# Key parts copied straight to their rows of the stack, in 16 SBUF-to-SBUF transfers a batch

## The chip, the cores and the metric

The kernel runs on one core of a Trainium2 chip. The core has TensorE (matrix products), VectorE, ScalarE and GpSimd (work on rows of up to 128 partitions), SyncE, which here only issues transfers, and 16 DMA engines, which carry them. Everything between engines is ordered by semaphores that the program sets and waits for. The metric is device time in microseconds of one execution, as the median of several.

## What is computed

32 sequences of 112 tokens with 256 features (`x`) attend to contexts of 375 tokens (`ctx_1024`) and then pass a second layer. Cut to what matters for the change, which is the first half, the cross-attention with 16 heads of 16 dims:

```python
qh = _split_heads(layernorm(x) @ wq + bq)        # 32 x 16 heads x 112 x 16
kh = _split_heads(ctx @ wk + bk)                 # 32 x 16 heads x 375 x 16
vh = _split_heads(ctx @ wv + bv)
logits = jnp.einsum('bhqd,bhkd->bhqk', qh, kh) / jnp.sqrt(jnp.float32(D))
attn = jax.nn.softmax(logits + mask * -1e9, axis=-1)
x = x + jnp.tanh(g_xattn[0]) * (merge_heads(attn @ vh) @ wo + bo)
x = x + jnp.tanh(g_ffn[0]) * second_layer(layernorm(x))   # routed attention with experts
```

## The kernel before

`prepare` loads weights and constants, `cross` is the first half (all 32 batches of the cross-attention), `switch` the second layer. The change is in `cross` alone. All loops are unrolled; `batches` (L315) calls an engine's `body` once a batch, and each engine's program is an order written out by hand. TensorE's `body` (L501) mixes four batches' worth of work: the scores of batch b (`S_`, one matmul a head, L437), the turned probabilities and their product with the values (`turn` L446, `weigh` L460), the end of batch b - 1 (`heads_back`, `heads_turn`, `project`), and the context transposes, keys and queries of batch b + 2.

A score keeps float32 precision by splitting. Keys and queries are each written as a sum of three bf16 parts, and one matmul over 128 rows adds eight products of parts: `K_stack` and `Q_stack` hold, for each head, eight blocks of 16 rows (D = 16 dims). `STACKED = ((0, 3, 1), (3, 3, 2), (6, 2, 0))` says it: blocks 0 to 2 hold key parts 0, 1, 2, blocks 3 to 5 again, blocks 6 and 7 parts 0 and 1; the third number picks the query parts.

The key parts come into being with feature on partition: `k_parts[P, 2, PARTS, EC, S2]`, two tiles (EC = 2) of 128 features, with features ordered dim first and head second, 375 keys of 2 bytes = 750 B in a row. ScalarE copies the keys out of PSUM and rounds the first part (`key_copy` L616, k_parts at L624), GpSimd takes the rest (`key_rest` L861), ScalarE rounds the second (`key_second` L644), VectorE takes the third (`key_third` L770, L772) and sets `k_split`. The stack needs dim on partition and head beside it. Queries go the same way (`split_queries` L774, last step L783, `q_split`).

That move is done by `exchange` (L330) on SyncE, through DRAM. For batch b and buffer p: wait for `k_split`, store the key parts to `k_dram` (L334); wait for `q_split`, two stores to `q_dram` (L336, L337); wait until the scores of batch b - 2 are done with the buffer (L339) and the key store has landed (L340); three loads into `K_stack` (L342; 48, 48 and 32 rows, 12,000 B each); wait for the query stores, three loads into `Q_stack` (L346; 3584 B a row). SyncE's `body` (L368) puts the context load of batch b + 4 (L45, L46) ahead of the exchange of batch b + 2, and eight loads of `x` in between. TensorE waits for all six stack loads ahead of a batch's first score (L434). ScalarE's `key_copy` waits for `k_stored` before it overwrites `k_parts` (L622), and `query_copy` for `q_stored`. Buffers of keys, stacks and values are double.

Of the kernel before, what the change touches and what calls it, by code (L numbers as in the profile page):

```python
# [13 lines left out]
BF16 = mybir.dt.bfloat16  # L14
# [4 lines left out]
P = 128  # L19
# [8 lines left out]
PARTS = 3  # L28
Q_COPIES = 5
STACKED = ((0, 3, 1), (3, 3, 2), (6, 2, 0))  # L30
# [11 lines left out]
def load_ctx(sp, z, c, rows, p):  # L42

    full = (z.KC - 1) * P
    sp.dma_start(c.ctx_in[:, p, 0:z.KC - 1, :], rows[0:full].rearrange("(k p) e -> p k e", p=P)).then_inc(c.ctx_loaded[p], 16)  # L45
    sp.dma_start(c.ctx_in[0:z.KL, p, z.KC - 1, :], rows[full:z.S2]).then_inc(c.ctx_loaded[p], 16)  # L46


def flat(ap):

    return ap.rearrange("a s e -> (a s) e")
# [203 lines left out]
def cross(nc, z, d, c):  # L255
    B, S, E, EC, H, G, KC, KP, S2, D = z.B, z.S, z.E, z.EC, z.H, z.G, z.KC, z.KP, z.S2, z.D
    NG = H // G
    STACK_LOADS = 16 * 2 * len(STACKED)
    VW = 32
    o = c.o  # L260
    with ExitStack() as ctx:
        sb = lambda name, shape, dt=F32: ctx.enter_context(nc.sbuf_tensor(name, shape, dt))
        ps = lambda name, shape: ctx.enter_context(nc.psum_tensor(name, shape, F32))
        sem = lambda name: ctx.enter_context(nc.semaphore(name))
# [5 lines left out]
        k_parts = sb("k_parts", [P, 2, PARTS, EC, S2], BF16)  # L270
        K_stack = sb("K_stack", [P, 2, H, S2], BF16)
# [22 lines left out]
        k_ready, k_copied = sem("k_ready"), sem("k_copied")  # L294
        va_ready, vb_ready, v_copied = sem("va_ready"), sem("vb_ready"), sem("v_copied")
        k_rest_done, k_second, k_split = sem("k_rest_done"), sem("k_second"), sem("k_split")
        k_stored = [sem(f"k_stored{i}") for i in range(2)]
        stack_loaded = [sem(f"stack_loaded{i}") for i in range(2)]
        half_set = sem("half_set")
        stats_done, moments_done, eps_added, rstd_done, xn_done, xbias_done = (  # L300
            sem(n) for n in ("stats_done", "moments_done", "eps_added", "rstd_done", "xn_done", "xbias_done"))
# [3 lines left out]
        wt_ready, wt_copied = sem("wt_ready"), [sem(f"wt_copied{i}") for i in range(2)]  # L305
        turns, turn_banks = weight_turns(z, c), [bank_s[0], bank_s[1], bank_o]
        q_dram = nc.dram_tensor("q_dram", (B, Q_COPIES, E, S), BF16).ap()
        k_dram = nc.dram_tensor("k_dram", (B, PARTS, E, S2), BF16).ap()
        scores_ready, scores_read, shift_done = sem("scores_ready"), sem("scores_read"), sem("shift_done")
        turned, exp_done, pv_done = sem("turned"), sem("exp_done"), sem("pv_done")  # L310
        headsT_copied, heads_ready, recip_done, heads_done = sem("headsT_copied"), sem("heads_ready"), sem("recip_done"), sem("heads_done")
# [13 lines left out]
        @block.sync  # L325
        def _(sp):
            def load(b, p):
                load_ctx(sp, z, c, flat(d.ctx[bass.ds(b, 1)]), p)

            def exchange(b, p, i):  # L330

                by_partition = lambda t: t.rearrange("a q (t p) n -> p (a q) t n", p=P)
                sp.wait_ge(k_split, b + 1)
                sp.dma_start(by_partition(k_dram[bass.ds(b, 1)]), k_parts[:, p, :, :, :]).then_inc(k_stored[p], 16)  # L334
                sp.wait_ge(q_split, b + 1)
                sp.dma_start(by_partition(q_dram[bass.ds(b, 1), 0:PARTS]), q_parts[:, :, :, :]).then_inc(q_stored[p], 16)  # L336
                sp.dma_start(by_partition(q_dram[bass.ds(b, 1), PARTS:Q_COPIES]), q_parts[:, 0:Q_COPIES - PARTS, :, :]).then_inc(q_stored[p], 16)  # L337
                if not (isinstance(b, int) and b < 2):
                    sp.wait_ge(scores_ready, H * (b - 1))  # L339
                sp.wait_ge(k_stored[p], 16 * i + 16)  # L340
                for j, n, first in STACKED:
                    sp.dma_start(K_stack[j * D:(j + n) * D, p, :, :].rearrange("d h k -> d (h k)"),  # L342
                                 k_dram[bass.ds(b, 1), 0:n].rearrange("a q (d h) k -> (a q d) (h k)", h=H)).then_inc(stack_loaded[p], 16)
                sp.wait_ge(q_stored[p], 32 * i + 32)
                for j, n, first in STACKED:
                    sp.dma_start(Q_stack[j * D:(j + n) * D, p, :, :].rearrange("d h s -> d (h s)"),  # L346
                                 q_dram[bass.ds(b, 1), first:first + n].rearrange("a q (d h) s -> (a q d) (h s)", h=H)).then_inc(stack_loaded[p], 16)


            def load_x(g):  # L350
                if g == 1:
                    sp.wait_ge(wt_ready, len(turns))
                first = g * z.GX
                sp.dma_start(c.X[0:S, first:first + z.GX, :], d.x[first:first + z.GX].rearrange("b s e -> s b e")).then_inc(c.x_loaded[g], 16)

            rows = lambda w: w.rearrange("h d c -> (h d) c").rearrange("(m p) c -> p m c", p=P)
            for load_no, (dst, src) in enumerate(((c.wq_in, d.wq2), (c.wk_in, d.wk2), (c.wv_in, d.wv2))):
                sp.dma_start(dst[:, :, :], rows(src)).then_inc(c.weights_loaded[load_no], 16)
            sp.dma_start(c.wg_in[:, 0, :], d.ws.rearrange("h e c -> (h e) c")).then_inc(c.weights_loaded[3], 16)
            sp.dma_start(c.wg_in[:, 1, :], d.wd.rearrange("h e c -> (h e) c")).then_inc(c.weights_loaded[3], 16)  # L360
            for f in range(EC):
                sp.dma_start(c.wo_in[:, f, :, :], d.wo2[:, f * P:(f + 1) * P, :].rearrange("e f d -> f e d")).then_inc(c.weights_loaded[3], 16)
            for b in range(2):
                exchange(b, b, 0)
                sp.wait_ge(ctxT_ready, b + 1)
                load(b + 2, b)

            def body(b, p, i, load_next=True):  # L368

                if load_next:  # L370
                    sp.wait_ge(ctxT_ready, b + 3)
                    load(b + 4, p)
                exchange(b + 2, p, i + 1)
                if b + 1 < B // z.GX:
                    load_x(b + 1)

            for p in range(2):
                body(p, p, 0)
            for b in range(2, B - 4):
                body(b, b % 2, b // 2)  # L380
            for p in range(2):
                body(B - 4 + p, p, B // 2 - 2, False)

        @block.tensor
        def _(pe):
# [45 lines left out]

            def scores(b, p, i, h, first):
                if h == 0:
                    pe.wait_ge(stack_loaded[p], STACK_LOADS * i + STACK_LOADS)  # L434
                if not (first and h < 2):
                    pe.wait_ge(scores_read, H * b + h - 1)
                nc.tensor.matmul(bank_s[h % 2][0:S, 0:S2], Q_stack[:, p, h, :], K_stack[:, p, h, :],  # L437
                                 start=True, stop=True).then_inc(scores_ready, 1)
# [62 lines left out]
            def body(b, p, i, first, ahead, last):  # L501


                back, front = not first, not last
                S_ = lambda *hs: [scores(b, p, i, h, first) for h in hs]
                S_(0, 1)
                if back:
# [101 lines left out]
        def _(act):  # L609
# [6 lines left out]
            def key_copy(b, p, i, t):  # L616

                act.wait_ge(k_ready, EC * b + t + 1)
                if t == 0 and not (isinstance(b, int) and b == 0):
                    act.wait_ge(k_split, b)  # L620
                    if not (isinstance(b, int) and b == 1):
                        act.wait_ge(k_stored[p], 16 * i)  # L622
                for dst in (k32[:, t, :], k_parts[:, p, 0, t, :]):
                    act.activation(dst, bank_ab[:, t, 0:S2], ACT.Identity, bias=c.bk[:, t:t + 1]).then_inc(k_copied, 1)  # L624

# [859 lines left out]
def flamingo_kernel(nc, ins, out):  # L1485
# [5 lines left out]
    with ExitStack() as ctx:  # L1491
# [11 lines left out]
        with ExitStack() as inner:  # L1503
            sb1 = lambda name, shape: inner.enter_context(nc.sbuf_tensor(name, shape, F32))
            c.ctx_in = sb1("ctx_in", [z.KP, 2, z.KC, z.E])
            c.ctx_loaded = [inner.enter_context(nc.semaphore(f"ctx_loaded{i}")) for i in range(2)]
            c.ctx_cleared = inner.enter_context(nc.semaphore("ctx_cleared"))
            c.x_loaded = [inner.enter_context(nc.semaphore(f"x_loaded{i}")) for i in range(z.B // z.GX)]
            c.vo_loaded = inner.enter_context(nc.semaphore("vo_loaded"))
            c.wq, c.wk, c.wv, c.wo = (sb1(n, [P, z.EC, z.E]) for n in ("wq_sb", "wk_sb", "wv_sb", "wo_sb"))  # L1510
            c.bq, c.bk = sb1("bq_sb", [P, z.EC]), sb1("bk_sb", [P, z.EC])
            c.bv, c.bo = sb1("bv_sb", [z.KP, z.E]), sb1("bo_sb", [z.S, z.E])
            c.maskb = sb1("maskb", [z.S, z.S2])

            free = z.B
            places = []
            for n in (z.M2, z.M2, z.X * z.D2 // P, 2, z.X * z.D2 * z.EC // z.E):
                free -= n
                places.append(c.X[:, free:free + n, :])
            c.wq_in, c.wk_in, c.wv_in, c.wg_in, wo_in = places  # L1520
            c.wo_in = wo_in.rearrange("p (f a) (x d) -> p f (a x) d", f=z.EC, d=z.D2)
            assert free >= z.GX
            c.weights_loaded = [inner.enter_context(nc.semaphore(f"weights_loaded{i}")) for i in range(4)]
            prepare(nc, z, d, c)
            cross(nc, z, d, c)
# [25 lines left out]
```

## Time and profile before

| | |
|---|---|
| median of 3 runs | 1317.49 us (1315.44 to 1321.64) |
| the profiled execution | 1307.75 us |
| its span, first to last instruction | 1306.0 us |
| TensorE busy | 1250.1 us, 96% |
| VectorE busy | 860.6 us, 66% |
| ScalarE, GpSimd busy | 612.0 and 549.9 us |
| DMA, the hardware queue | 262,788 packets, 197.64 MB, 66.7% of 16 engines |
| mean granted TensorE clock | 0.986 |

Busy times of engines overlap. The span is cut into 40 slices of 32.65 us; a digit is the busy share of a slice in tenths. The first half lasts until slice 20. All durations in the rows come from this one execution, which is 9.7 us under the median of the runs.

### The profile page before, as it was taken

The page shows a single profiled execution, that of the slowest core. Times are in us where ns is not written, and L with a number is a line of the kernel's source. Part 1 is how long each engine was busy: PE and PEld are TensorE (multiplying, and loading weights), DVE is VectorE, ACT ScalarE, POOL GpSimd, SP SyncE. Part 2 cuts the span into 40 slices and gives each one's busy share as a digit, 9 for nine tenths or more (in the row PEclk, how much of TensorE's full clock was granted, in tenths as well). Part 3 has the DMA queues.
Part 4 walks back from the last instruction along what each step waited for, and adds up shares of the span by engine and source line. Part 5 has one row for each costly group of instructions (what it writes and reads, how often), then busy time and mean ns, then how long its engine had stood idle before and what let it go on. Part 6 is the DMA issues. An engine that isn't in the chain of part 4 may idle for free. (4 is left out here: it accounts for less than half of the span.)

```text
span 1306.0 us, 40359 instructions
## 1 busy us (share of the span) xinstructions
PE 1250.1 (96%) x15928; PEld 1019.9 (78%) x15928; DVE 860.6 (66%) x2455; ACT 612.0 (47%) x1353; POOL 549.9 (42%) x823
## 2 busy tenths in 40 slices
PE   5799999999999999999988999999999999999996
PEld 4577777777777777777767888888888888888885
DVE  2566766766776776766655676677667667766652
ACT  3455555556556556556423443443444344344431
POOL 3476676676676676666620221221222122122211
PEclk9899999999999999999989999999999999999997
DMA  8898897787787787786404665566566656656563
GB/s 231 186 192 189 192 202 166 165 185 162 164 185 159 159 185 155 159 189 145 104 18 110 145 138 156 139 141 143 138 143 138 157 136 141 142 139 148 138 156 91
DMA packets 262975, 200.21 MB, mean 153 GB/s; under 512 B 195906, under 2 KB 243844, under 8 KB 258692
## 3 DMA queue, kind: packets, MB, share of 16 engines
q1 hardware_dynamic: 262788, 197.64, 66.7%
q8 instruction: 127, 2.08, 0.7%
q14 instruction: 60, 0.49, 0.1%
HBM read 125.49 MB, written 72.11 MB: 151 GB/s over the span
## 5 line engine op out<-in xcount | busy, mean ns | idle before, releaser
L858 POOL TENSOR_SCALAR shifted<-raw,neg_max 112x375 f32<-112x375 f32 x512 | 304.5, 603 | 197.1 <-DVE neg_max L741 131.4
L741 DVE CUSTOM_DVE_ANT_0 raw<-bank_s,maskb 112x375 f32<-112x375 f32 x512 | 269.0, 544 | 119.4 <-issue 77.9
L653 ACT ACTIVATE probsT<-bank_t 128x448 f32<-128x448 f32 x384 | 181.1, 547 | 162.9 <-PE bank_t L446 162.9
L446 PE MATMUL bank_t<-ident,shifted 112*128 112x112 f32 x1536 | 170.7, 261 | 4.1 <-POOL shifted L858 4.1
L446 PEld LDWEIGHTS bank_t<-ident,shifted 112*128 112x128 f32 x1536 | 156.3, 141 | 22.7 <-POOL shifted L858 19.8
L437 PE MATMUL bank_s<-K_stack,Q_stack 128*112 128x375 bf16 x512 | 158.4, 337 | 12.8 <-DVE neg_max L741 8.2
L1381 DVE TENSOR_REDUCE max<-bank_s 112x4 f32<-112x448 f32 x128 | 78.7, 615 | 78.1 <-PE bank_s L1140 78.1
L1454 POOL TENSOR_TENSOR mix_bd<-pm_te,tok 128x448 f32<-128x448 f32 x32 | 30.4, 951 | 214.8 <-DMA pm_te<-pm_dram 214.8
L1092 PE MATMUL bank_ab<-xnT,wk2T 128*128 128x224 f32 x512 | 110.9, 360 | 0.6 <-ACT kT L1281 0.6
L1092 PE MATMUL bank_ab<-xnT,wq2T 128*128 128x224 f32 x512 | 110.8, 360 | 0.4 <-ACT qT L1273 0.4
L201 POOL TENSOR_SCALAR var_eps<-moments 112x1 f32<-112x1 f32 x32 | 7.1, 223 | 233.4 <-DVE moments L197 233.2
L1092 PEld LDWEIGHTS bank_ab<-xnT,wq2T 128*128 128x128 f32 x512 | 95.6, 192 | 12.1 <-issue 8.4
L1092 PEld LDWEIGHTS bank_ab<-xnT,wk2T 128*128 128x128 f32 x512 | 95.1, 192 | 11.7 <-issue 7.6
L460 PE MATMUL bank_o<-probsT,V 128*32 128x112 f32 x3072 | 101.6, 264 | 0.1
L460 PEld LDWEIGHTS bank_o<-probsT,V 128*32 128x32 f32 x3072 | 69.5, 110 | 39.5 <-issue 28.1
L437 PEld LDWEIGHTS bank_s<-K_stack,Q_stack 128*112 128x112 bf16 x512 | 62.9, 130 | 44.4 <-DVE neg_max L741 22.6
L404 PE MATMUL bank_ab<-ctxT,wk_sb 128*128 128x375 f32 x256 | 93.8, 491 | 1.2 <-ACT ctxT L614 1.2
L428 PE MATMUL bank_ab<-wv_sb,ctxT 128*128 128x256 f32 x372 | 90.4, 379 | 0.0
L1384 DVE TENSOR_TENSOR shifted<-bank_s,max 112x448 f32<-112x448 f32 x128 | 79.9, 624 | 4.4
L428 PEld LDWEIGHTS bank_ab<-wv_sb,ctxT 128*128 128x128 f32 x372 | 68.7, 190 | 6.6
L1164 PEld LDWEIGHTS bank_g<-v,probsT 112*64 112x64 f32 (+1 forms) x1792 | 57.8, 131 | 19.7 <-issue 19.7
L1281 ACT ACTIVATE kT<-bank_ab 128x448 f32<-128x448 f32 x64 | 34.8, 543 | 75.2 <-PE bank_ab L1092 75.2
(141 smaller groups left out, 2227.4 us busy)
## 6 DMA issues: line engine op xcount, KB each, us to landing
K_stack<-k_dram SPq DMA_DIRECT2D x64, 562.5 KB, 7.3
k_dram<-k_parts SPq DMA_DIRECT2D x32, 562.5 KB, 5.0
att_dram<-att_q SPq DMA_DIRECT2D x32, 511.0 KB, 4.1
att_th<-att_dram SPq DMA_DIRECT2D x32, 511.0 KB, 4.3
v_dram<-mv SPq DMA_DIRECT2D x32, 455.0 KB, 6.1
v<-v_dram SPq DMA_DIRECT2D x32, 455.0 KB, 4.0
K_stack<-k_dram SPq DMA_DIRECT2D x32, 375.0 KB, 9.4
Q_stack<-q_dram SPq DMA_DIRECT2D x64, 168.0 KB, 9.3
```

The source lines that it names most:

```text
L404: last = nc.tensor.matmul(bank_ab[:, t, 0:S2], c.wk[:, e, t * P:(t + 1) * P], ctxT[:, p, e, 0:S2], start=(e == 0), stop=(e == EC - 1))
L428: last = nc.tensor.matmul(dst, ctxT[:, p, e, k * KP:(k + 1) * KP], c.wv[:, e, :], start=(e == 0), stop=(e == EC - 1))
L437: nc.tensor.matmul(bank_s[h % 2][0:S, 0:S2], Q_stack[:, p, h, :], K_stack[:, p, h, :], start=True, stop=True).then_inc(scores_ready, 1)
L446: last = nc.tensor.transpose(bank_t[0:KP, k, j * S:(j + 1) * S], shifted[:, g % 2, j, k * KP:(k + 1) * KP], c.ident[0:S, 0:S])
L460: last = nc.tensor.matmul(bank_o[j * VW:(j + 1) * VW, g * S:(g + 1) * S], V[:, p, k, G * g + j, :], probsT[:, g % 2, k, j * S:(j + 1) * S] ...
L653: act.activation(probsT[:, g % 2, k, :], bank_t[0:KP, k, 0:G * S], ACT.Exp).then_inc(exp_done, 1)
L741: dve.tensor_tensor_reduce(raw[:, g % 2, j, :], bank_s[h % 2][0:S, 0:S2], c.maskb[:, :], -1.0, -LEAST, ALU.add, ALU.min, neg_max[:, g % 2, ...
L858: pool.tensor_scalar(shifted[:, g % 2, j, 0:S2], raw[:, g % 2, j, :], -1.0, neg_max[:, g % 2, j:j + 1], ALU.mult, ALU.add).then_inc(shift_ ...
L1092: last = nc.tensor.matmul(bank_ab[:, 0, m * 2 * S:(m + 1) * 2 * S], w, xnT[:, e, 2 * h:2 * h + 2, :].rearrange("p r s -> p (r s)"), start= ...
L1164: last = nc.tensor.matmul(weighed(half, m)[lo:hi, :], probsT[:, half, m, lo:hi], v[:, p, 2 * G * half + m, :], start=True, stop=True)
L1381: dve.tensor_reduce(neg_max[:, g % 2, :], sc, AXX, ALU.max).then_inc(max_done, 1)
L1384: dve.tensor_tensor(shifted[:, g % 2, :, :], sc, neg_max[:, g % 2, :].unsqueeze(2).to_broadcast([S, G, S]), ALU.subtract).then_inc(shift_d ...
```

## The change

The DRAM tensor `k_dram`, the store into it and the three loads of `K_stack` go. In their place SyncE issues 16 transfers a batch from `k_parts` to `K_stack`, one for each block (8) and tile of features (2): 128 partitions of 750 B go to 8 rows of 16 heads x 375 keys. The first six (blocks 0 to 2) are issued before SyncE waits for `q_split`, the other ten behind the two query stores and ahead of the query loads. The wait for the scores of batch b - 2 moves to the front of `exchange`. `stack_loaded` becomes two pairs of semaphores, one for keys and one for queries; TensorE waits for both, and ScalarE's `key_copy` waits for the keys' one instead of `k_stored`.

```diff
-    STACK_LOADS = 16 * 2 * len(STACKED)
+    DH = P // H
+    KEY_LOADS, QUERY_LOADS = 16 * EC * sum(n for _, n, _ in STACKED), 16 * len(STACKED)
...
-        k_dram = nc.dram_tensor("k_dram", (B, PARTS, E, S2), BF16).ap()
...
                 by_partition = lambda t: t.rearrange("a q (t p) n -> p (a q) t n", p=P)
+                if not (isinstance(b, int) and b < 2):
+                    sp.wait_ge(scores_ready, H * (b - 1))
                 sp.wait_ge(k_split, b + 1)
-                sp.dma_start(by_partition(k_dram[bass.ds(b, 1)]), k_parts[:, p, :, :, :]).then_inc(k_stored[p], 16)
+
+                def stack_keys(blocks):
+                    for j, n, _ in blocks:
+                        for part in range(n):
+                            for t in range(EC):
+                                row = (j + part) * D + t * DH
+                                sp.dma_start(K_stack[row:row + DH, p, :, :],
+                                             k_parts[:, p, part, t, :]).then_inc(keys_stacked[p], 16)
+
+                stack_keys(STACKED[:1])
                 sp.wait_ge(q_split, b + 1)
                 sp.dma_start(by_partition(q_dram[bass.ds(b, 1), 0:PARTS]), q_parts[:, :, :, :]).then_inc(q_stored[p], 16)
                 sp.dma_start(by_partition(q_dram[bass.ds(b, 1), PARTS:Q_COPIES]), q_parts[:, 0:Q_COPIES - PARTS, :, :]).then_inc(q_stored[p], 16)
-                if not (isinstance(b, int) and b < 2):
-                    sp.wait_ge(scores_ready, H * (b - 1))
-                sp.wait_ge(k_stored[p], 16 * i + 16)
-                for j, n, first in STACKED:
-                    sp.dma_start(K_stack[j * D:(j + n) * D, p, :, :].rearrange("d h k -> d (h k)"),
-                                 k_dram[bass.ds(b, 1), 0:n].rearrange("a q (d h) k -> (a q d) (h k)", h=H)).then_inc(stack_loaded[p], 16)
+                stack_keys(STACKED[1:])
                 sp.wait_ge(q_stored[p], 32 * i + 32)
...
-                    pe.wait_ge(stack_loaded[p], STACK_LOADS * i + STACK_LOADS)
+                    pe.wait_ge(keys_stacked[p], KEY_LOADS * (i + 1))
+                    pe.wait_ge(queries_stacked[p], QUERY_LOADS * (i + 1))
...
-                        act.wait_ge(k_stored[p], 16 * i)
+                        act.wait_ge(keys_stacked[p], KEY_LOADS * i)
```

## Rows read from the trace of the kernel before

**Rows 1.** Page: TensorE's busy time; TensorE and DMA in 40 slices
```profile
PE 1250.1 (96%) x15928; PEld 1019.9 (78%) x15928; DVE 860.6 (66%) x2455; ACT 612.0 (47%) x1353; POOL 549.9 (42%) x823
...
PE   5799999999999999999988999999999999999996
...
DMA  8898897787787787786404665566566656656563
```

**Rows 2.** Busy us (x instructions) of engines in a stretch, clock, DMA share, GB/s
```profile
core 0: us, PE busy (x) PEld busy (x) DVE busy (x) ACT busy (x) POOL busy (x), PEclk, DMA share, GB/s
...
260.00:400.00 140.00, 138.38 (x1465) 110.73 (x1466) 97.54 (x326) 81.02 (x174) 95.58 (x146) 1.00 0.79 169
```

**Rows 3.** Waits from 100 to 640 us: us in total, times, longest
```profile
PEld bank_o L460 <- issue: 24.5, 57, 0.5
PEld bank_s L437 <- DVE neg_max L741: 19.2, 55, 0.9
```

**Rows 4.** Timeline of TensorE: start, us, what; score matmuls around a batch's begin
```profile
253.57 0.61 PE L437 MATMUL bank_s<-K_stack,Q_stack 128*112 128x375 bf16 x2
...
256.57 0.53 PE L437 MATMUL bank_s<-K_stack,Q_stack 128*112 128x375 bf16 x2
...
275.99 0.53 PE L437 MATMUL bank_s<-K_stack,Q_stack 128*112 128x375 bf16 x2
```

**Rows 5.** The same view: first scores of batch 0 and of batch 1
```profile
41.49 0.50 PE L437 MATMUL bank_s<-K_stack,Q_stack 128*112 128x375 bf16 x2 [4.31 <-DMA Q_stack<-q_dram]
...
62.05 0.53 PE L437 MATMUL bank_s<-K_stack,Q_stack 128*112 128x375 bf16 x2
```

**Rows 6.** Timeline of SyncE over one period: transfers as issued
```profile
252.93 0.38 SPq L334 DMA_DIRECT2D k_dram<-k_parts  x1
259.65 0.38 SPq L336 DMA_DIRECT2D q_dram<-q_parts  x1
...
260.83 1.40 SPq L342 DMA_DIRECT2D K_stack<-k_dram  x3
262.73 1.25 SPq L346 DMA_DIRECT2D Q_stack<-q_dram  x3
264.02 0.42 SPq L45 DMA_DIRECT2D ctx_in<-in_ctx_dram  x1
```

**Rows 7.** Timeline of VectorE: last thirds of the key and query splits
```profile
251.88 1.02 DVE L772 TENSOR_TENSOR k_parts<-k,k_parts 128x750 bf16<-128x750 f32 x1
...
259.24 0.39 DVE L783 TENSOR_TENSOR q_parts<-q_rest,q_parts 128x224 bf16<-128x224 f32 x1
```

**Rows 8.** DMA issues of the run: KB each, median us to landing
```profile
k_dram<-k_parts SPq DMA_DIRECT2D x32, 562.5 KB, 5.0
...
q_dram<-q_parts SPq DMA_DIRECT2D x32, 168.0 KB, 2.4
...
q_dram<-q_parts SPq DMA_DIRECT2D x32, 112.0 KB, 2.6
Q_stack<-q_dram SPq DMA_DIRECT2D x32, 112.0 KB, 9.8
```

**Rows 9.** DMA view of 260 to 454.2 us, ten periods
```profile
DMA packets 28488, 32.78 MB, mean 169 GB/s; under 512 B 14470, under 2 KB 25900, under 8 KB 27180
...
q1 hardware_dynamic: 28460, 32.42, 77.0%
...
k_dram<-k_parts SPq DMA_DIRECT2D x10, 562.5 KB, 4.8
```

**Rows 10.** Stretches: weight loads, key loads (two batches), key store; last number GB/s
```profile
17.00:22.00 5.00, 5.00 (x20) 3.60 (x18) 0.91 (x3) 2.07 (x4) 1.63 (x2) 1.00 1.10 348
243.50:250.50 7.00, 7.00 (x74) 5.45 (x76) 3.88 (x15) 4.65 (x10) 5.31 (x8) 1.00 0.99 207
262.90:269.90 7.00, 7.00 (x74) 5.46 (x76) 3.86 (x15) 4.66 (x10) 5.24 (x8) 1.00 1.00 199
254.00:255.00 1.00, 1.00 (x7) 0.90 (x7) 0.97 (x4) 0.54 (x2) 0.88 (x3) 1.00 1.02 314
```

**Rows 11.** Stretches between the halves: TensorE's busy us first, clock third from last
```profile
664.00:668.00 4.00, 1.62 (x14) 0.82 (x14) 2.67 (x7) 0.90 (x2) 0.00 (x0) 0.81 0.00 0
668.00:672.00 4.00, 3.13 (x7) 1.95 (x8) 1.49 (x8) 0.23 (x1) 0.25 (x1) 0.50 0.00 0
```

More of the change, by code:

```diff
@@ L296, in cross @@
         k_rest_done, k_second, k_split = sem("k_rest_done"), sem("k_second"), sem("k_split")
-        k_stored = [sem(f"k_stored{i}") for i in range(2)]
-        stack_loaded = [sem(f"stack_loaded{i}") for i in range(2)]
+        keys_stacked = [sem(f"keys_stacked{i}") for i in range(2)]
+        queries_stacked = [sem(f"queries_stacked{i}") for i in range(2)]
         half_set = sem("half_set")
@@ L346, in exchange @@
                     sp.dma_start(Q_stack[j * D:(j + n) * D, p, :, :].rearrange("d h s -> d (h s)"),
-                                 q_dram[bass.ds(b, 1), first:first + n].rearrange("a q (d h) s -> (a q d) (h s)", h=H)).then_inc(stack_loaded[p], 16)
+                                 q_dram[bass.ds(b, 1), first:first + n].rearrange("a q (d h) s -> (a q d) (h s)", h=H)).then_inc(queries_stacked[p], 16)
             def load_x(g):
```

## The prediction

> **What bounds the kernel now.** I read the page first. TensorE is busy 96% of the span and no other engine over 66%, and the slices split at about 655 us into two halves: the cross-attention, where the 16 DMA engines are busy 70 to 90%, and the second layer, where they are less so [rows 1]. The change touches only the first half, so I took a stretch of 140 us out of it: TensorE 98.8% busy at full clock, the DMA engines 79% [rows 2]. TensorE is the bound, DMA is second with about a fifth of its time free. The waits of this half say the same: no wait for a stack is among those of 100 to 640 us, and TensorE's weight loads wait for 24.5 us at the most for any one thing in these 540 us [rows 3].
>
> Then one period. The first score matmul of a batch comes at 256.57 and of the next at 275.99: 19.42 us a batch [rows 4]. There are 31 such steps from batch 0 (41.49) to batch 31 (41.49 + 20.56 + 30 x 19.42 = 644.7) [rows 4, 5]. SyncE in that period [rows 6]: the key store at 252.93, right behind the last third of the split [rows 7], two query stores from 259.65, three key loads from 260.83, three query loads from 262.73, two context loads. The last query load starts at about 263.5 and takes 9.8 us to land [rows 6, 8], so the stack is whole at about 273.3 and used at 275.99: 2.7 us to spare. That small reserve, and the DMA time a batch, are what the change plays with.
>
> **What it removes.** Per batch one store of 576,000 B (0.38 us of SyncE, 4.8 to 5.0 us to landing) and three loads, eight parts of 192,000 B, 1.536 MB in all [rows 6, 8, 9]. The loads hold the DMA engines full at 199 and 207 GB/s [rows 10], so 1.536 MB / 203 GB/s = 7.6 us; the store runs at 314 GB/s [rows 10], 1.8 us. The DMA engines were 77% busy over ten periods [rows 9], 15.0 us a batch. Keys are 9.4 of that, all other transfers 5.5 us (queries, context, small fetches). On SyncE 0.38 + 1.40 us go.
>
> **What it adds.** 16 transfers a batch, each 128 pieces of 750 B = 96,000 B, from 128 partitions into 8 rows of K_stack (8 of the dims, 16 heads in each). SyncE: single issues last 0.38 to 0.42 us [rows 6], so 16 x 0.42 = 6.7 us instead of 1.8. SyncE issues for about 4.6 us of 19.42 now (11 transfers, from the same rows); 9.5 us still fits, and I cost it at nothing, since the waits for the splits cover it. Queued on SyncE behind the moved wait for the scores are the six first copies, the query stores and the next context load; the scores it waits for end at 254.18 (start 253.57, 0.61 us) [rows 4], 1.3 us after the old store was issued, and the query split is not there before 259.6 [rows 7], so the move costs nothing by itself. Three other edits have one answer: the split semaphores cost TensorE one more wait a batch that passes; the wait for k_parts in the key copy on ScalarE is now for a stack which TensorE has used before that copy anyway; the query stores now run behind six copies instead of behind nothing.
>
> The price that matters is the DMA time of a copy, and no row shows an SBUF-to-SBUF transfer. Two things have to be read.
>
> First, how many engines it uses. Ten periods have 14,470 packets under 512 B [rows 9]. The query stores are 280 KB a batch [rows 8] in pieces of 224 B (112 bf16), 1280 packets; that leaves 167 a batch, the tiny packets with which an engine reports its share. Eleven transfers are issued a batch, so ten of them have 16 and one has 7. The one is the context's last 119 rows, which have no larger divisor up to 16 than 7. An 8-row target should so get 8 engines. The Trainium skill says so too (DMA: Bandwidth & Descriptors, "Why a DMA increments its semaphore by 16 and not by 1": the largest number up to 16 that divides the slowest dimension of both sides); by this rule the trace's 7 is right, and a copy here has 8.
>
> Second, how fast 8 rows take data. Weight loads into 128 rows run at 348 GB/s, key loads into 32 or 48 rows at 199 to 207 with the engines as full [rows 10]. Fewer target rows are slower, though the key pieces are far larger (12,000 B against 1024 B). Bounds for a copy: at best the rate per engine of the key store, 314 / 16 = 19.6 GB/s, on 8 engines: 0.61 us. At worst the rate per row of the key loads, 203 / 32 = 6.3 GB/s, on 8 rows, 51 GB/s: 1.9 us. A gain is left out at the lower end: 16 copies at 0.61 us are 9.8 us on each of the eight engines, against 9.4 us for store and loads. I take 1.2 us: the engines don't wait for each other between copies, so part of them is already in the next copy's 8 rows; with two copies always open it would be 0.95, with one 1.9, and I expect it nearer to two. It is nearer to the row on key loads, which is the only one with few target rows.
>
> The Trainium skill bears on this against the change (SBUF — State Buffer, "Door 1: The DMA port swizzle"): four neighbouring partitions share a port of 27.2 GB/s, so 8 rows have two, 54 GB/s, 1.76 us a copy, and 48 or 32 rows have 8 ports, 218 GB/s. The trace's 199 to 207 GB/s against 348 agrees with it. By that figure alone the period would be 16 x 1.76 + 5.5 = 33.7 us, close to the second rival.
>
> **The sum.** DMA time a batch on the eight engines: 16 x 1.2 + 5.5 = 24.7 us, over TensorE's 19.42. The reserve goes first, and then DMA sets the period. The chain of one batch gives less: query split 3.1 us after the batch's start, store about 3, ten copies 12, query loads and landing 4, in all 22. So 31 x 24.7 - 603.2 = +162.5 us. At the start batch 0 already waits 4.31 us for the query stack, queued behind the keys [rows 5]; its keys now take 19.2 instead of 9.4 + about 1.5 us between store and load: +8. Profiled execution: 1307.75 + 170.5 = 1478. Its span is 1306.0, with 1.75 around it. The median of the runs shown is 1317.49, 9.7 over the profiled one; on that scale 1488.
>
> The clock: behind the first half TensorE is busy 1.62 of 4 us, and the granted clock goes to 0.81 and then 0.50, the lower level of 1.2 GHz, for some 8 us [rows 11]. With 5 us of waiting a batch the same may come back, and costs at most 4 us of work per spell; it fits into the period that DMA sets, so I add nothing.
>
> **Rivals.** (a) The copies stay in step: all eight engines write into the same 8 rows at a time, 1.6 to 1.9 us each. Period 31.1 to 35.9 us, sum with the start +376 to +529, 1693 to 1847. For it: they start together and have equal shares. Against: there is no bar between copies, and an engine that is ahead finds the next 8 rows free. (b) The other side: the copies are hidden. It decides at (19.42 - 5.5) / 16 = 0.87 us a copy, and with the reserve of 2.7 us and the later query loads at about the same. At 0.61 us DMA falls to 15.3 us on eight engines, TensorE stays the bound, and only the start can move, by the 4.31 us it waits: 1313 to 1322. For it: 750 B pieces ran at 19.6 GB/s per engine, no DRAM round trip any more. Against: all those had 128 rows on one side. The same would come if a copy went to 16 engines and rows were no limit: the change's gain would still be off the path. (c) Just over the edge, 0.9 to 1.0 us: period 19.9 to 21.5, +17 to +68, 1334 to 1386. (d) Faster by over 0.5%: nothing on TensorE's path is taken away; the start offers 4.31 us, under the bound.
>
> **How the numbers follow.** About 0.5% (6.6 us) is what a measurement of this kernel can tell from no change. Forecast (1.0 to 1.5 us a copy, period 21.5 to 29.5, 1386 to 1642): 0.50. (a) and what lies between: 0.18. (b): 0.21. (c): 0.08. (d): 0.03. Faster 0.03, same 0.21, slower 0.76. The range reaches down to (b) and up to a period of 31.3: 1312 to 1700. The likeliest case alone is 1386 to 1642.
>
> **What would show it.** First the period between first score matmuls: 19.42 refutes me, 24.7 is the forecast. TensorE's wait before the first score matmul must be put down to the stack's DMA, above all Q_stack, as the keys are in front of it. GB/s in the first half falls from 169, while packets of 750 B grow from 768 to 2048 a batch. The tiny packets a batch should be 10 less 4, plus 16: 6 x 16 + 7 + 16 x 8 = 231; were it 359, the copies use 16 engines. The time from a copy's issue to its landing tells its price; SyncE issues much longer than 0.42 us tell of a queue that is full. Wrong I'd be if 8 rows take data at over 110 GB/s, or if engines spread so well that the copies cover all rows at once.

## The result, and the profile after

The changed kernel takes 1436.62 us (median of 4 runs, 1414.19 to 1442.38) against 1319.57 us before (4 runs, 1315.44 to 1324.36). Ratios in this document leave out runs that lie over 1.5% above the fastest of their kernel, so this one goes by 1414.19 and 1434.42 us: 1.078 times as long, 95% interval 1.072 to 1.084. It is slower, as forecast, by less than forecast (1488). The profiled execution is the one of 1438.82 us, with a span of 1437.1.

The page of the changed kernel: TensorE's busy time, then TensorE, its granted clock and DMA in 40 slices (of 35.9 us now), and the DMA queue.

```profile
PE 1277.2 (89%) x15928; PEld 1042.5 (73%) x15928; DVE 868.5 (60%) x2455; ACT 614.1 (43%) x1353; POOL 551.4 (38%) x823
...
PE   5498998797896999897966899999999999999996
...
PEclk9699999898998999998987999999999999999996
DMA  7677777666766666766560466566566655666663
...
q1 hardware_dynamic: 301700, 179.21, 62.6%
```

TensorE, which was full from slice to slice [rows 1], now has gaps through the first half and none to speak of in the second. The DMA engines are *less* busy than before (7s and 6s instead of 8s), and they carry 18 MB less. So neither engine is full by this page, and yet the first half is longer. That is what an average over 16 DMA engines hides when eight of them do the work.

TensorE's timeline (start, us, what, idle before): the first scores of batches 0, 9 and 10, and of batch 31.

```profile
58.38 0.85 PE L444 MATMUL bank_s<-K_stack,Q_stack 128*112 128x375 bf16 x2 [13.03 <-DMA Q_stack<-q_dram]
...
250.14 0.50 PE L444 MATMUL bank_s<-K_stack,Q_stack 128*112 128x375 bf16 x2 [3.11 <-issue]
...
279.56 0.85 PE L444 MATMUL bank_s<-K_stack,Q_stack 128*112 128x375 bf16 x2 [9.95 <-issue]
...
759.87 0.85 PE L444 MATMUL bank_s<-K_stack,Q_stack 128*112 128x375 bf16 x2 [8.40 <-issue]
```

Against [rows 4, 5] this gives the account. Batch 0 starts at 58.38 instead of 41.49: +16.9 us. The 31 steps to batch 31 take 701.5 us, 22.63 each, instead of 645.79 - 41.49 = 604.3 us, 19.49 each: +97.2 us. What lies behind batch 31's start takes 677.2 instead of 660.2: +17.0. Together the 131.1 us between the spans. (The medians are 117.1 us apart, nearer to the first two parts, 114.1 us, than to all three.) The steps aren't alike: the shortest are 19.4 us, as before, and the longest 30.1. The waits ahead of a batch's first score have a DMA as releaser only in the first row; the others say "issue", that is, nothing that the profile could tie to them. What they waited for has to be read from the other queues, and from the times at which the trace has the transfers landing.

SyncE in the step from 250.14 to 279.56:

```profile
253.20 0.40 SPq L347 DMA_DIRECT2D q_dram<-q_parts  x1
253.65 1.10 SPq L348 DMA_DIRECT2D q_dram<-q_parts  x1
254.79 6.53 SPq L342 DMA_DIRECT2D K_stack<-k_parts  x10
261.36 1.45 SPq L352 DMA_DIRECT2D Q_stack<-q_dram  x3
...
267.18 11.72 SPq L342 DMA_DIRECT2D K_stack<-k_parts  x6
```

The last of the three query loads in that row, as the DMA view of 261 to 263 us has it (us to landing):

```profile
Q_stack<-q_dram SPq DMA_DIRECT2D x1, 112.0 KB, 17.1
```

It lands at 279.5, and the first score of batch 10 starts at 279.56. In 20 of the 32 batches the first score starts 0.09 to 0.14 us after the last query load has landed: batches 9, 10 and 31 above, with their waits marked "issue", are among them. Averaged over the steps from batch 1 to batch 31, the first query store is issued 3.17 us after a batch's first score, the first query load 8.62 us later, the last one has landed after 10.42 us more, and the next first score follows 0.50 us behind. The query loads are late because they stand behind the copies.

And stretches of that step (busy us of PE, PEld, DVE, ACT, POOL; then clock, DMA share, GB/s):

```profile
258.00:262.00 4.00, 4.00 (x50) 3.56 (x50) 2.31 (x9) 2.88 (x7) 3.13 (x5) 1.00 0.58 52
...
269.00:271.00 2.00, 0.60 (x24) 0.36 (x16) 0.09 (x1) 0.92 (x3) 0.00 (x0) 1.00 0.74 57
271.00:273.00 2.00, 0.00 (x0) 0.00 (x0) 0.00 (x0) 0.00 (x0) 0.00 (x0) 0.85 0.58 51
273.00:275.00 2.00, 0.00 (x0) 0.00 (x0) 0.00 (x0) 0.00 (x0) 0.00 (x0) 0.50 0.58 53
```

The ten copies are issued by 261.3 and the query loads behind them at 261.36 to 262.8, with 17 us to go. But the queue moves 51 to 57 GB/s where it moved 199 to 207 before [rows 10], at a DMA share of 0.58, little more than eight engines of 16. At 51 to 57 GB/s a copy of 96,000 B takes 1.7 to 1.9 us. The next six issues last 11.72 us, 1.95 each on the mean instead of 0.65: SyncE itself is held up. That the queue in front of it is full is my reading of that; no view shows the queue's depth. All compute engines stand still from 271 to 275, and TensorE's clock falls to 0.50.

The same copies to the same rows aren't always so slow. At the start of the same step:

```profile
251.00:253.00 2.00, 2.00 (x29) 1.75 (x31) 1.93 (x7) 1.77 (x4) 1.29 (x2) 1.00 0.54 147
```

Each copy ends with eight packets of 4 B, one from each engine that took part (counted in experiment 3); the trace has the time of every packet. From 256.7 to 262.4 they come in four groups of eight, each group within 0.3 us, about 1.8 us from one to the next: the engines are in step. From 250 to 253.5 they come evenly spread: the engines are apart, and nearly three times as much goes through.

### The profile page after: what moved, and what is told of

Same layout as the page of the kernel before. It is cut to its first block and busy times, and to the rows that moved or that the text cites. A ratio compares the mean times of both kernels' runs of the same rounds, so it can differ in the third digit from the quotient of the medians.

```text
span 1437.1 us, 40743 instructions
## 1 busy us (share of the span) xinstructions
PE 1277.2 (89%) x15928; PEld 1042.5 (73%) x15928; DVE 868.5 (60%) x2455; ACT 614.1 (43%) x1353; POOL 551.4 (38%) x823
## 5 line engine op out<-in xcount | busy, mean ns | idle before, releaser
L444 PE MATMUL bank_s<-K_stack,Q_stack 128*112 128x375 bf16 x512 | 163.9, 349 | 100.3 <-issue 80.5
L453 PE MATMUL bank_t<-ident,shifted 112*128 112x112 f32 x1536 | 181.0, 271 | 4.2 <-POOL shifted L865 4.2
L453 PEld LDWEIGHTS bank_t<-ident,shifted 112*128 112x128 f32 x1536 | 166.0, 147 | 24.2 <-POOL shifted L865 18.6
L1171 PEld LDWEIGHTS bank_g<-v,probsT 112*48 112x48 f32 (+1 forms) x1792 | 58.6, 133 | 19.7 <-issue 18.8
L1171 PE MATMUL bank_g<-v,probsT 112*48 112x65 f32 (+1 forms) x1792 | 67.7, 227 | 2.2 <-ACT probsT L1305 1.8
```

The costliest lines, as they stand in the source:

```text
L453: last = nc.tensor.transpose(bank_t[0:KP, k, j * S:(j + 1) * S], shifted[:, g % 2, j, k * KP:(k + 1) * KP], c.ident[0:S, 0:S])
L1171: last = nc.tensor.matmul(weighed(half, m)[lo:hi, :], probsT[:, half, m, lo:hi], v[:, p, 2 * G * half + m, :], start=True, stop=True)
```

## The experiments

The theory under test, **P**: four neighbouring rows of SBUF share one inlet for transfers, rows r and r + 32 too, and what costs is that a copy's 8 rows side by side have only two inlets for eight engines; how much it costs hangs on whether the engines stay in step. The rivals: **E**, eight engines instead of 16, or the price of a 750 B piece between SBUF and SBUF; **S**, SyncE's issues or the moved wait; and that only the number of target rows counts, wherever they lie. Experiments 1 to 6 were executed once each. Runs of the two kernels with the changed kernel's copies spread over 28 and 38 us (experiment 8), those of the kernel before over 11, so only a difference clearly over that counts.

**1. Rows 4 apart.** Only the target rows of the 16 copies change. The query stack keeps its order, so this kernel's scores aren't those of the reference.

```diff
-                                row = (j + part) * D + t * DH
-                                sp.dma_start(K_stack[row:row + DH, p, :, :],
+                                n16 = (j + part) * EC + t
+                                rows = slice(32 * (n16 // 4) + n16 % 4, 32 * (n16 // 4) + n16 % 4 + 29, 4)
+                                sp.dma_start(K_stack[rows, p, :, :],
```

> The 16 key copies keep their order, size and count, only their 8 target rows lie 4 apart (rows r, r+4, ... r+28) instead of side by side. The query stack keeps its old order of rows, so the scores aren't those of the reference; the work is the same. Theory P (four neighbouring rows share one inlet, so 8 rows side by side have two): eight inlets now, no queue at any, a copy costs about 0.6 us on its eight engines, 16 x 0.6 + 5.5 = 15.1 us a batch, under TensorE's 19.4. Mean period of batches 19.4 to 19.8 us (22.5 in the changed kernel), time 1310 to 1345. Theory E (8 of 16 engines, or the price of a 750 B piece between SBUF and SBUF, is what costs): rows don't matter, mean period stays 22.5, time 1415 to 1440.

Measured: 1316.67 us, against 1305.76 for the kernel before on the same chip. The steps are back; 8.1 of the 8.9 us between this span and that of the profile before lie behind batch 31's start. First scores of batches 0 and 31, and the stretch in which the ten copies run:

```profile
41.95 0.84 PE L445 MATMUL bank_s<-K_stack,Q_stack 128*112 128x375 bf16 x2 [4.02 <-DMA Q_stack<-q_dram]
...
646.61 0.53 PE L445 MATMUL bank_s<-K_stack,Q_stack 128*112 128x375 bf16 x2
...
263.00:269.00 6.00, 6.00 (x65) 4.87 (x64) 3.05 (x11) 4.30 (x10) 4.84 (x8) 1.00 0.50 134
```

(646.61 - 41.95) / 31 = 19.51 us a step. The last query load now lands 5.22 us on the mean after the first is issued (10.42 in the changed kernel), and 3.33 us are to spare before the next first score. With the same eight engines (share 0.50), sizes and number of copies, 134 GB/s go through instead of 51 to 57. E falls, and so does the idea that 8 target rows as such are slow.

**2. Rows 2 apart.** The same edit with `slice(16 * (n16 // 2) + n16 % 2, 16 * (n16 // 2) + n16 % 2 + 15, 2)`; its scores aren't those of the reference.

> As the rows 4 apart, but 2 apart: r, r+2, ... r+14, so four inlets by theory P, two engines at each. Scores aren't those of the reference either. P: at worst 16 copies of 0.88 us = 14.1 + 5.5 = 19.6 us a batch: mean period 19.4 to 20.3. E: 22.5. A theory by which only neighbours as such disturb each other would give the same as 4 apart, with no burst slower than there; P wants bursts of copies at half the rate that 4 apart reaches, when all eight engines are in step.

Measured: 1383.12 us; first scores at 49.01 and 718.41, so 21.59 us a step. A miss for my number (at most 20.3), on the side of P's order: 22.63 side by side, 21.59 at 2 apart, 19.51 at 4 apart; but with one execution and the spread of these kernels, 2 apart and side by side can't be ranked. The stretch of 258 to 263 has 126 GB/s, that of 270 to 274 has 111 at a share of 0.50. The other sign that I had asked for, bursts at half of experiment 1's 134 GB/s, isn't there: the slowest 3 us with copies alone carried 84. So twice the inlets weren't worth as much as I had reckoned. In writing the number I had only looked at one copy by itself; here two copies in a row have the *same* four inlets, which experiment 5 takes up.

**3. Sixteen engines.** Each copy goes from 128 partitions to the same 128 partitions; the stack then holds the wrong layout, and the scores aren't those of the reference.

```diff
-                                row = (j + part) * D + t * DH
-                                sp.dma_start(K_stack[row:row + DH, p, :, :],
+                                sp.dma_start(K_stack[:, p, (j + part) * EC + t, :],
```

> The 16 copies go from 128 partitions to the same 128 partitions of K_stack, copy c into the place of head c, so each has all rows and should get 16 engines; same bytes, pieces and count of issues, but the stack holds the wrong layout and the scores aren't those of the reference. P and E both: mean period 19.4, the K copies done in 5 to 8 us. A theory S, by which the 16 issues on SyncE or the moved wait set the period, gives 22.5. Tiny packets a batch should be 359 here against 231 in the changed kernel.

Measured: 1309.87 us; first scores at 42.66 and 646.70, 19.49 us a step. The number of engines can be read from ten steps (260 to 454.2) of each kernel, this one first and then the one with rows 4 apart:

```profile
DMA packets 41766, 26.95 MB, mean 139 GB/s; under 512 B 16364, under 2 KB 40456, under 8 KB 41736
```

```profile
DMA packets 40513, 26.94 MB, mean 139 GB/s; under 512 B 15101, under 2 KB 39204, under 8 KB 40484
```

Less the 1280 query pieces a batch, 356 and 230 tiny packets are left: 359 and 231 were what 16 and 8 engines a copy call for. (The changed kernel has as many packets in all as the one with rows 4 apart, 301,700.) With 16 issues, the moved wait and the SBUF-to-SBUF path all in place nothing is lost, so S falls as well.

**4. The wait in front.** The kernel before, with only the wait for the scores moved ahead of the key store.

```diff
+                if not (isinstance(b, int) and b < 2):
+                    sp.wait_ge(scores_ready, H * (b - 1))
                 sp.wait_ge(k_split, b + 1)
                 sp.dma_start(by_partition(k_dram[bass.ds(b, 1)]), k_parts[:, p, :, :, :]).then_inc(k_stored[p], 16)
...
-                if not (isinstance(b, int) and b < 2):
-                    sp.wait_ge(scores_ready, H * (b - 1))
```

> The kernel before with one edit of the change alone: the wait for the scores of batch b - 2 moved to the front of the exchange, key store and loads still through DRAM. My step says it costs nothing: the store is issued 1.3 us later, it lands before the loads are issued. Period 19.42, time within 0.5% of before. A theory that the later start eats the reserve of 2.7 us gives some tenths of a us a batch: period 19.6 to 20, 1323 to 1335.

Measured: 1307.58 us against 1305.76, 0.14% more; first scores at 42.01 and 646.50, 19.50 us a step. The moved wait costs nothing that one execution can show.

**5. Rows 2 apart, other order.** The same rows and inlets for each copy as in experiment 2, but the next copy goes to other rows' inlets (with one exception a batch: row 32 and then row 1, if rows r and r + 32 share one). Its scores aren't those of the reference.

```diff
-                    for j, n, _ in blocks:
-                        for part in range(n):
-                            for t in range(EC):
-                                n16 = (j + part) * EC + t
-                                rows = slice(16 * (n16 // 2) + n16 % 2, 16 * (n16 // 2) + n16 % 2 + 15, 2)
-                                sp.dma_start(K_stack[rows, p, :, :],
+                    for t in range(EC):
+                        for j, n, _ in blocks:
+                            for part in range(n):
+                                row = 16 * (j + part) + t
+                                sp.dma_start(K_stack[row:row + 15:2, p, :, :],
```

> As the rows 2 apart, same rows and inlets for each copy, but another order: there, copies followed each other in pairs at the same four inlets; here each next copy goes to the next group of 16 rows. Scores aren't those of the reference. P with engines that run ahead: an engine that is ahead now finds free inlets, so the engines draw apart and the mean period falls from 21.6 to 19.4 to 20.5. If the order doesn't matter and only the number of inlets of a copy does: 21.2 to 22.0.

Measured: 1314.84 us. Two stretches of 100 to 600 us, of experiment 2 and of this one:

```profile
100.00:600.00 500.00, 458.09 (x4749) 367.49 (x4750) 314.95 (x1040) 259.53 (x554) 307.21 (x464) 0.96 0.69 131
```

```profile
100.00:600.00 500.00, 493.10 (x5295) 394.89 (x5294) 350.25 (x1158) 286.61 (x616) 339.62 (x514) 1.00 0.66 144
```

TensorE is full again (493.10 of 500 us; the kernel before had 493.19), and the steps take 19.63 us, (654.03 - 45.48) / 31. No size, count, row or engine differs, only which copy follows which; the two executions are 68 us apart, more than any spread seen here. That is what P with engines that run ahead of each other says, and what no theory on the single copy can say.

**6. Rows 16 apart.** `slice(n16, n16 + 113, 16)`; its scores aren't those of the reference.

> The 8 target rows of a copy 16 apart, over all 128 partitions. Scores aren't those of the reference. If each group of four neighbouring rows had an inlet of its own (32 of them), eight inlets take part and this is like 4 apart: period 19.4. The Trainium skill (SBUF, State Buffer, Door 1) has row r and r + 32 at one port and 16 ports in all: rows 16 apart then reach four ports, two engines at each, and four copies in a row go to the same four. By that 21 to 23 us. If only neighbourhood mattered: 19.4.

Measured: 1402.04 us; first scores at 50.66 and 735.33, 22.09 us a step. The rows lie further apart than in experiment 1, and it is slower: distance doesn't help, the number of inlets does. It agrees with the Trainium skill's map (SBUF — State Buffer, "Door 1: The DMA port swizzle"), by which these 8 rows reach four ports, and four copies in a row the same four.

**7. Side by side, in pairs.** The target rows of the changed kernel, complete and with its outputs, in an order that should be the worst: seven pairs of copies, the second of each to rows 32 further on, and two copies by themselves.

```diff
-                    for j, n, _ in blocks:
-                        for part in range(n):
-                            for t in range(EC):
-                                row = (j + part) * D + t * DH
-                                sp.dma_start(K_stack[row:row + DH, p, :, :],
-                                             k_parts[:, p, part, t, :]).then_inc(keys_stacked[p], 16)
+                    for n16 in ((0, 4, 1, 5, 3, 2) if blocks[0][0] == 0 else (6, 7, 8, 12, 9, 13, 10, 14, 11, 15)):
+                        row, part, t = n16 * DH, n16 // EC % PARTS, n16 % EC
+                        sp.dma_start(K_stack[row:row + DH, p, :, :],
+                                     k_parts[:, p, part, t, :]).then_inc(keys_stacked[p], 16)
```

> The changed kernel with its target rows side by side as they are, but the copies in another order: where one can, each is followed by the copy whose rows lie 32 further on (0 and 4, 1 and 5, 2 and 6, 8 and 12, and so on), which by theory P has the same two inlets. Complete and with the reference's scores. P with engines that run ahead: the one ahead finds the next rows' inlets taken by the rest, so the engines draw apart less; mean period above the 22.4 to 22.6 of the two profiled runs of the old order, 24 to 31 us, time 1450 to 1680. If order matters only by chance: 22 to 23, 1370 to 1442.

Measured: 1531.56 us (4 runs, 1516.94 to 1542.92), 1.163 times the kernel before (1.156 to 1.170). First scores:

```profile
62.93 0.85 PE L442 MATMUL bank_s<-K_stack,Q_stack 128*112 128x375 bf16 x2 [15.48 <-DMA Q_stack<-q_dram]
...
868.90 0.85 PE L442 MATMUL bank_s<-K_stack,Q_stack 128*112 128x375 bf16 x2 [7.15 <-issue]
```

(868.90 - 62.93) / 31 = 26.00 us a step, and none under 23.8. The order alone, at the same rows, moves the kernel by some 100 us (the medians are 95 us over the changed kernel's and 126 over experiment 8's, on different chips). The order was made on the ground that rows r and r + 32 share an inlet; this result and experiment 6 both speak for it. That the engines go in step more, as I had argued, it doesn't show: a 750 B packet takes longer (87 ns on the mean against 71 in the changed kernel), but copies whose eight closing packets come within 0.4 us and clear of others are rarer (10 of 480 against 39).

**8. `k_dram` kept.** The changed kernel with the unused DRAM tensor still declared, to ask after the 17 us behind batch 31.

```diff
+        k_dram = nc.dram_tensor("k_dram", (B, PARTS, E, S2), BF16).ap()
```

> The changed kernel with the unused DRAM tensor k_dram still declared, so that the tensors behind it in DRAM lie where they lay before. The profiled run of the changed kernel spent 677 us behind batch 31's start, the kernel before 660, though no line there is changed. If the place in DRAM does it, this one has 660 there and 1405 to 1420 in all. If it is a disturbance of that one run, the place changes nothing: anything from 660 to 677, and the time is that of the changed kernel, 1414 to 1442.

Measured: 1405.24 us (4 runs, 1370.27 to 1408.07). Batch 31 starts at 745.32, and 661.0 us follow. By itself this would speak for the place in DRAM; but the kernels of experiments 1 to 3 and 5 to 7 have no `k_dram` either, and have 659.1 to 668.3 us there. So the 17 us aren't of the change. In that one trace the second layer's transfers take longer: `v_dram<-mv` lands after 7.4 us, in the kernel before after 6.1 and in all nine experiments after 6.0 to 6.3, and TensorE waits 11.8 us in all for `mix_bd` (1.3 before). Whether that comes from the execution or from where it ran isn't shown; the kernel before took 1315 to 1324 us beside the changed kernel and 1304 to 1315 beside this one. This kernel is also the best view of the two ways in which the same code can run. Two stretches:

```profile
260.00:454.20 194.20, 187.17 (x2002) 150.21 (x1992) 132.30 (x437) 107.83 (x232) 128.04 (x194) 0.99 0.67 135
...
600.00:745.00 145.00, 111.22 (x1144) 89.14 (x1136) 75.10 (x249) 58.35 (x126) 71.58 (x109) 0.89 0.64 99
```

In the first the steps take 19.4 to 20.6 us, but for one of 22.8, and 135 GB/s go through; in the second they take 21 to 29 us at 99 GB/s, with the DMA engines about as busy. That it is the state of the engines against each other which differs, and lasts for many batches, fits this, the wide spread of its runs (38 us over 4, where the kernel before has 11 over 12 on that chip) and the two experiments on order. But the trace doesn't name the engine of a packet. That engines go in step for some us and apart for others is seen in the closing packets (the result section); that this is what makes the long steps, and what brings it about, is inferred.

**9. Both stacks 4 apart.** The complete kernel: experiment 1, with the queries brought into the same order of rows.

```diff
+PLACE = (0, 1, 3, 2, 4, 5, 6, 7)
+Q_FIRST = (1, 2, 3, 0)
...
-                                row = (j + part) * D + t * DH
-                                sp.dma_start(K_stack[row:row + DH, p, :, :],
+                                g, c = divmod(PLACE[j + part], 2)
+                                row = 32 * g + EC * c + t
+                                sp.dma_start(K_stack[row:row + 4 * DH - 3:4, p, :, :],
...
-                for j, n, first in STACKED:
-                    sp.dma_start(Q_stack[j * D:(j + n) * D, p, :, :].rearrange("d h s -> d (h s)"),
-                                 q_dram[bass.ds(b, 1), first:first + n].rearrange("a q (d h) s -> (a q d) (h s)", h=H)).then_inc(queries_stacked[p], 16)
+                for g, first in enumerate(Q_FIRST):
+                    sp.dma_start(Q_stack[32 * g:32 * g + 32, p, :, :].rearrange("d h s -> d (h s)"),
+                                 q_dram[bass.ds(b, 1), first:first + 2].rearrange("a q (t d h) s -> d (a q) t (h s)", h=H, t=EC)).then_inc(queries_stacked[p], 16)
```

> The complete kernel with both stacks in the new order of rows: each key copy's 8 target rows lie 4 apart, and the queries come in four loads of 32 rows in the same order (8 engines each, pieces of 3584 B). P (inlets of four neighbouring rows), now with the first four runs behind it: period 19.4, first score at 42, time as the kernel before within 0.5% (ratio 0.997 to 1.006). It can't be faster by more than the start's 4 us, since TensorE's work is the same. If the query loads on 8 engines or their four issues eat what is left of the reserve: period 19.5 to 20.5, 1325 to 1355.

Measured: 1310.14 us (10 runs) against 1309.41 (12 runs), ratio 1.0019, interval 0.9997 to 1.0041. The copies without DRAM in between cost nothing when they are laid out so, and gain nothing:

```profile
100.00:600.00 500.00, 493.10 (x5299) 394.86 (x5298) 348.31 (x1155) 288.82 (x620) 340.05 (x514) 1.00 0.52 144
```

The DMA share falls from 0.80 to 0.52 in this stretch, and TensorE's 493.10 us of 500 are the 493.19 of before. A third of the DMA engines' busy time is taken away, off the path.

## Why the prediction was right, and where its sizes were off

- **What bounds the kernel before.** Right. DMA was second, with a fifth free; with the layouts of experiments 1, 3, 5 and 9 TensorE stays the bound and the time as it was, with those of 2, 6 and 7 the steps get longer.
- **Eight engines a copy.** Right, counted in experiment 3. The rule of the Trainium skill (DMA: Bandwidth & Descriptors, "Why a DMA increments its semaphore by 16 and not by 1") agrees with both counts. But it isn't the eight engines that cost: they have time for all of it in experiment 1.
- **The price of a copy.** The bounds of 0.61 and 1.9 us held in the stretches shown: 1.7 to 1.9 us where the engines are in step (51 to 57 GB/s), 0.65 us where they are apart (96,000 B at 147 GB/s). The estimate of 54 GB/s for two ports, from the Trainium skill's 27.2 GB/s a port (SBUF — State Buffer, "Door 1: The DMA port swizzle"), is the former. The upper bound was lucky: it took the rate per row from the third load's 32 rows, and the first two's 48 rows would have given 2.8 us. I also gave 48 rows eight ports; by the same map the second load's, 48 to 95, reach twelve. The value between, 1.2 us, was near: the 750 B packets between the first scores of batch 0 and 31 took 71 ns each on the mean, which at 16 to an engine is 1.14 us a copy (42 ns and 0.67 us with rows 4 apart). The reason I gave for it, that the next copy's rows are free for an engine which is ahead, turned out to matter most: experiments 5 and 7 change only that, by the order of copies. I had used it only to choose a number.
- **The sum.** Forecast 31 x 24.7 - 603.2 = +162.5, measured +97.2. The term that was mis-sized is the step, 24.7 us against 22.63, and less by the price of a copy than by what was added up: I took the DMA engines' busy times one after another as the step, and even at 1.14 us that gives 16 x 1.14 + 5.5 = 23.7. The chain of one batch, which I had reckoned at 22 us and set aside as the smaller, is what the landings show: 3.17 + 8.62 + 10.42 = 22.2 us from a first score to the landing of the queries for the next. Its total came out right with parts that were off in opposite directions: store and ten copies were 15 of it and query loads 4, measured 8.6 and 10.4, as the query loads are queued behind copies not yet done. Whether full engines or this chain set a step can't be told apart here, as each makes the other longer.
- **The start.** Forecast +8, measured +16.9. The step that failed is "the query stores now run behind six copies", which I had put among the edits with one answer. At the start nothing covers it. ScalarE's timeline has the queries of batch 1 waiting for batch 0's query store:

```profile
39.64 0.60 ACT L646 ACTIVATE q<-bank_ab,bq_sb 128x112 f32<-128x112 f32 x2 [5.97 <-DMA q_dram<-q_parts]
...
42.57 1.08 PE L579 MATMUL bank_s<-ident,X 128*128 128x128 f32 x4 [7.98 <-DVE wk2T L831]
```

  TensorE's turning of the second layer's weights waits 7.98 us behind it, for a copy that VectorE does after the split of those queries. The batch itself then waits 13.03 us for its query loads, issued at 41.42 behind ten copies whose issue took from 30.18 to 41.4. With rows 4 apart the same wait is 4.02 us and batch 0 starts at 41.95, so the start too is the price of the copies.
- **SyncE.** Issues cost more than the 0.42 us I took from single ones. Where nothing holds the queue, six copies in a row took 3.69 us (experiment 3) and 3.90 us (experiment 1): 0.62 to 0.65 each, 10 us a batch instead of 6.7. In those two kernels it was hidden all the same, as costed.
- **The moved wait.** Right at nothing (experiment 4).
- **The clock.** From 100 to 600 us the changed kernel has 446.19 us of TensorE in 500 at a mean clock of 0.96, where it had 493.19 at 1.00 (the kernel before first):

```profile
100.00:600.00 500.00, 493.19 (x5299) 394.93 (x5298) 348.12 (x1155) 288.68 (x620) 339.13 (x515) 1.00 0.80 173
```

```profile
100.00:600.00 500.00, 446.19 (x4640) 357.90 (x4641) 307.55 (x1018) 254.31 (x543) 299.68 (x454) 0.96 0.70 127
```

  At 22.63 us a step that is 20.2 us of matmuls a step instead of 19.2, so 1 us of work a step was added, which I put down to the clock, well under what I had allowed. Whether any of it reached the time isn't settled by these runs.
- **The rivals.** That the copies stay in step was right for stretches (257 to 262 us, in a step of 29.4) and wrong as a lasting state; even the order made for it came to 26.0, not to 31. The hidden case, too, came true in part: the same code has steps of 19.4 us, nine of the first 20 in experiment 8, beside those of 21 to 29.
- **Behind batch 31's start** I had forecast nothing, and 17.0 of the 131.1 us lie there. No other kernel shows more than 8.1 there, so I don't count them with the change.

## What to carry to other kernels

Look where a transfer's target rows lie before counting its bytes: eight rows side by side took 51 to 57 GB/s with the engines in step (147 with them apart), eight rows 4 apart 134. Where a contraction runs over the partitions, their order is free, and here a permutation of both operands cost nothing (ratio 1.002, experiment 9). And a mean DMA share of 0.6 or 0.7 doesn't mean that there is room: at a share of 0.58 eight of the engines could be full, and the queries queued behind the copies were what the next batch waited for.

## What was not expected of the hardware

- The order of copies alone, with the same rows, sizes and engines, decided between 19.6 and 21.6 us a step (rows 2 apart) and between about 22.5 and 26.0 (side by side).
- The same kernel (experiment 8) ran for batches at 19.4 us a step and then for batches at 21 to 29; its total spread over 38 us from run to run.
- An issue in a row of copies took SyncE 0.62 to 0.65 us on the mean, and 1.95 us on the mean in the row of six behind ten slow ones.
